# Expert stages of a transformer kernel: tokens sorted by expert through DRAM, 46 tiles of 256 places instead of eight dense experts

## The reference

```python
logits = x @ router_w.T                               # 8 experts
routing_weights, selected = sparsemixer_eval(logits)  # two experts a token
dense_w.at[tok, selected[:, k]].add(routing_weights[:, k])
for e in range(E):
    h = silu(x @ w_gate[e].T) * (x @ w_up[e].T)       # 128 -> 256
    out = out + dense_w[:, e:e + 1] * (h @ w_down[e].T)
```

## Time and profile before

| | us |
|---|---|
| median of 3 runs | 1792.99 (1792.24 to 1793.76) |
| span of the profiled execution | 1790.5 |
| PE busy | 1635.4 |
| DVE busy | 1373.5 |
| ACT busy | 997.7 |
| POOL busy | 342.6 |

### The profile page before, as it was taken

How to read it: one execution, slowest core, us unless ns; L and a number is a source line. 1 busy time by engine, 2 the same in 40 slices (tenths; PEclk the granted TensorE clock), 3 DMA queues, 4 the chain that set the end, 5 groups by cost and what they waited for, 6 DMA issues and landing times.

```text
span 1790.5 us, 30396 instructions
## 1 busy us (share of the span) xinstructions
PE 1635.4 (91%) x10929; PEld 954.7 (53%) x10929; DVE 1373.5 (77%) x2257; ACT 997.7 (56%) x1974; POOL 342.6 (19%) x742
## 2 busy tenths in 40 slices
PE   5899999978999999999999889999999687999687
PEld 5788888721111111111111237788888566666476
DVE  5755555689999999999999447655577796788895
ACT  3223323437888888888888863333322564655463
POOL 5311002462000001000000131001000134334221
PEclk9899999978999999999999999999999798999798
DMA  3000000121001010010001001000000000000000
GB/s 131 1 1 0 0 0 19 53 71 55 23 28 30 29 38 22 23 37 23 23 29 38 8 4 57 1 0 0 0 0 1 1 1 1 2 2 2 1 20 28
DMA packets 25302, 35.93 MB, mean 20 GB/s; under 512 B 5808, under 2 KB 19696, under 8 KB 24672
## 3 DMA queue, kind: packets, MB, share of 16 engines
q1 hardware_dynamic: 25184, 34.38, 6.4%
HBM read 22.57 MB, written 8.78 MB: 18 GB/s over the span
## 4 chain that ended last, share of the span: by engine, by line
PE 76%; DVE 11%; ACT 5%; issue 4%; POOL 2%; DMA 0%; SPq 0%; POOLq 0%; ACTq 0%; DVEq 0%
PE PS L971 14%; PE PS L440 12%; PE PS L959 10%; PE PS L429 7%; PE PS L430 6%; PE PS L431 6%; PE PS L948 5%; ACT probs L1043 3%; DVE neg_half L1106 3%; PE PS L1557 3%; PE PS L1645 2%; PE PS L1655 1%; PE PS L1588 1%; PE PS L1566 1%; PE PS L329 1%
## 5 line engine op out<-in xcount | busy, mean ns | idle before, releaser
L1106 DVE TENSOR_REDUCE neg_half<-PS 128x2 f32<-128x1024 f32 x512 | 601.5, 1219 | 39.5 <-PE PS L948 24.4
L1043 ACT ACTIVATE probs<-PS 128x512 f32<-128x512 f32 x1024 | 528.9, 603 | 112.3 <-PE PS L959 112.2
L523 ACT ACTIVATE shared<-PS 128x512 f32<-128x512 f32 x256 | 152.6, 597 | 374.1 <-PE PS L431 361.2
L959 PE MATMUL PS<-qk_all 51*128 51x512 bf16 x1024 | 279.7, 387 | 17.6 <-ACT probs L1043 12.4
L617 DVE TENSOR_TENSOR shared<-shared,PS 128x512 f32<-128x512 f32 x256 | 174.0, 686 | 156.2 <-ACT shared L523 154.5
L971 PE MATMUL PS<-probs,Vg 128*32 128x512 f32 x2048 | 274.5, 608 | 0.1
L440 PEld LDWEIGHTS PS<-wd,shared 128*128 128x128 f32 x2048 | 249.3, 193 | 11.2 <-issue 0.5
L959 PEld LDWEIGHTS PS<-qk_all 51*128 51x128 bf16 x1024 | 71.6, 93 | 338.3 <-ACT probs L1043 319.3
L440 PE MATMUL PS<-wd,shared 128*128 128x128 f32 x2048 | 250.7, 276 | 0.0
L948 PE MATMUL PS<-qk_all 48*128 48x512 bf16 x1024 | 193.8, 390 | 17.4 <-DVE neg_half L1106 15.3
L625 DVE SCALAR_TENSOR_TENSOR x<-PS,gates,x 128x128 f32 (+1 forms) x512 | 144.0, 343 | 71.6 <-PE PS L440 71.6
(11 more groups left out here) (213 smaller groups left out, 2061.2 us busy)
## 6 DMA issues: line engine op xcount, KB each, us to landing
split<-qk_all SPq DMA_DIRECT2D x16, 384.0 KB, 3.3
qk_all<-split SPq DMA_DIRECT2D x64, 96.0 KB
qk_all<-split SPq DMA_DIRECT2D x64, 64.0 KB
qk_all<-split SPq DMA_DIRECT2D x64, 32.0 KB
shared<-OTs SPq DMA_DIRECT2D x60, 32.0 KB
probs<-in_ret_const SPq DMA_DIRECT2D x1, 1538.5 KB, 6.8
qk_all<-negT SPq DMA_DIRECT2D x96, 4.0 KB, 1.7
SC<-inverse SPq DMA_DIRECT2D x3, 512.0 KB, 4.9
```

The lines of the kernel that those rows point to most:

```text
L523: act.activation(sg[:, f, :], bank(f), ACT.Silu).then_inc(s["silu"], 1)
L959: pe.matmul(bank(RING_AT + use % RING), qs[rows, slot, 1, pair, kt * P:(kt + 1) * P], qs[rows, slot, 0, pair, half * GW:(half + 1) * GW], ...
L1043: act.activation(probs[:, n % 2, STRIPS * strip + pair, :], bank(RING_AT + use % RING), ACT.Exp, scale=ATT_SCALE).then_inc(s["exped"], 1)
L1106: dve.tensor_reduce(neg_half[m % 2][:, i % 2, :, at], bank(use_bank(i, m), 2).rearrange("p (s w) -> p s w", s=STRIPS), AX.X, ALU.max, nega ...
```

## The change

Each expert stage is cut into two parts of 2048 tokens. For each part DVE routes, PE counts the members of each expert with two matmuls, and DVE turns the counts into a place for each token and choice: each expert gets whole tiles of 256 places, 23 tiles a part in every case, 46 a stage. POOL scatters the normalised tokens (`tokens_all`) by indirect DMAs into rows of a DRAM array `slots_x`, one DMA for each token tile and choice, 32 a part. Then each tile runs through one expert: SP reads the expert's number into a register, fetches that expert's weights (384 KB) into a ring of three, and loads the tile's rows (128 KB); PE turns them, runs gate and up as 4 plain fp32 matmuls of 256 columns and down as 4 of 128 columns; ACT copies the result out, and SP stores it to `slots_y`. POOL gathers the two results of each token by indirect DMAs (8 a group, 64 a stage), and DVE adds them to `x` with their weights (`moe_add`). The dense weights in SBUF, their high and low parts and the loops over groups and experts are gone; the tiles are written out.

The second part's gathers and adds are moved: those of stage 0 into turn 0 of the attention, those of stage 2 into the feed-forward stage. Groups 4 to 7 are normalised for the attention by DVE (`LATE_TOKENS`) in place of POOL.

```diff
+SLOTS_TILE = 256
+PARTS_MOE = 2
+PART_TILES = (2 * PART_TOKENS + EXPERTS * (SLOTS_TILE - 1)) // SLOTS_TILE
+STAGE_TILES = PARTS_MOE * PART_TILES
+RING_TILES = 3
...
+        def moe_scatter(pool, n, part, lo=0, hi=PART_TOKEN_TILES):
+            pool.wait_ge(moe["place"], parts_before(n) + part + 1)
+            for t in range(part * PART_TOKEN_TILES + lo, part * PART_TOKEN_TILES + hi):
+                for k in range(2):
+                    pool.indirect_dma_start(slots_x[part][:, :], bass.IndirectOffsetOnAxis(place[:, k, t:t + 1], 0),
+                                            tokens_all[:, t, :], None).then_inc(moe[f"scattered{part}"], 16)
...
+        def moe_load_weights(sp, n, i):
...
+            e = sp.value_load(expert_of[0:1, part, i % PART_TILES:i % PART_TILES + 1], min_val=0, max_val=EXPERTS - 1)
+            wait(sp, moe["y_ps"], k - RING_TILES + 1)
+            sp.dma_start(w_ring[:, r, :], a["w_experts"][bass.ds(e, 1), :, :].rearrange("o p w -> (o p) w")).then_inc(moe[f"w{r}"], 16)
...
+        def moe_store_slots(sp, n, i):
...
+            sp.wait_ge(moe["y"], k + 1)
...
+        def moe_sp(sp, n, at_tile=None, between=None):
+            AHEAD = RING_TILES - 1
...
+            for i in range(STAGE_TILES):
+                if i + AHEAD < STAGE_TILES:
+                    moe_load_weights(sp, n, i + AHEAD)
+                    moe_load_slots(sp, n, i + AHEAD)
+                moe_store_slots(sp, n, i)
...
         def moe_pe(pe, n):
...
+            for i in range(STAGE_TILES):
+                if i + 2 < STAGE_TILES:
+                    turned(i + 2)
+                if i + 1 < STAGE_TILES:
+                    gate_up(i + 1)
+                down(i)
...
+        LATE_ADDS, LATE_TOKENS = {5: 4, 10: 5, 14: 6}, {7: 4, 12: 5, 15: 6}
...
+                if n == 3 and g < PART_GROUPS:
+                    moe_add(dve, 2, PART_GROUPS + g, "late")
```

More of the change, by code:

```diff
@@ L208, in macaron @@
         gn = sb("gn", [P, 2])
[L211 to L215, removed]
+        ld = stage_sems(ctx, nc, "ld", "fp4 ret wret x_first x_second x_rest small ident half att ones ident_b filled stored")
+        ln = stage_sems(ctx, nc, "ln", "stats link rstd late")
+        moe = stage_sems(ctx, nc, "moe", "xn xT_ps xT logit_ps logits shifted exped weighed members counts experts place scattered0 scattered1 "
+                         "w0 w1 w2 in0 in1 in2 out0 out1 out2 in_ps inT gu silu0 silu h y_ps y came0 came1 half_added x_acc")
+        att = stage_sems(ctx, nc, "att", "xn xT_ps xTf q_ps k_ps qkf_half v_ps v_raw qkf rest1 part2 parts V to_dram0 to_dram1 strips filled read neg_step "
                     "neg_p neg_rows scoredT exped pad Vg pv evac moved sums inverse spread moved_last rec on proj biased added neg")
@@ L361, in b @@
             def b(v):
                 return v.unsqueeze(2).to_broadcast([P, N, EXPERTS])
-            S, G, A, F, D, O1, O2, M = (v[:, t, :] for v in (scores, gates, size, factor, below, first, second, masked))
+            S, A, F, D, O1, O2, M = (v[:, t, :] for v in (scores, size, factor, below, first, second, masked))
             K, X = ([v[:, k, t, :] for k in range(2)] for v in (kept, shifted))
-            m, mu = ([v[:, k, t] for k in range(2)] for v in (largest, mult))
+            m = [largest[:, k, t] for k in range(2)]
@@ L403, in route @@
[L403 to L413, removed]
@@ L552, in moe_act, with result @@
+            def result(i):
+                k = tile_of(n, i)
+                act.wait_ge(s["y_ps"], k + 1)
+                wait(act, s[f"out{k % RING_TILES}"], 16 * (k // RING_TILES))
+                act.activation(slots_out[:, k % RING_TILES, :], bank(1)[:, 0:SLOTS_TILE], ACT.Copy
+                               ).then_inc(s["y"], 1)
+            if n == 0:
+                for g in range(HEAD_GROUPS):
+                    moe_copy(act, n, g)
             moe_exp(act, n, 0)
+            for g in range(HEAD_GROUPS, GROUPS):
+                moe_copy(act, n, g)
@@ L554, in moe_act @@
+            moe_exp(act, n, 1)
             act.activation(sg[:, 0, 0:1], ident[:, 0:1], ACT.Silu).then_inc(s["silu0"], 1)
-            act.wait_ge(s["silu0"], 1)
-            group(0, False)
-            with act.Fori(1, GROUPS - 2 if n == 0 else GROUPS - 1) as g:
-                group(g, False)
+            act.wait_ge(s["silu0"], n // 2 + 1)
+            turned(0)
+            turned(1)
+            silu(0)
+            for i in range(STAGE_TILES):
+                if i + 2 < STAGE_TILES:
+                    turned(i + 2)
+                if i + 1 < STAGE_TILES:
+                    silu(i + 1)
+                result(i)
+                if n == 0:
+                    prep_act_at(act, i - PART_TILES)
```

813 lines of the change are left out of this document (419 added, 394 removed).

## The result

The change makes the kernel slower: 2264.8 us (median of 4 runs, 2260.8 to 2269.4) against 1793.4 us, a ratio of 1.263 (95% interval 1.260 to 1.265). The forecast was 2334 us in a range of 2080 to 2530. The profiled execution has a span of 2259.0 us against 1790.5, so 468.5 us have to be found.

What follows compares the result with a forecast made beforehand. PE was taken as the bound. Tiles 984 less dense steps 648, plus heads 68 and 68, turn 0 49 and feed-forward 20, gave +541 us on a 1790.5 us span, about 2334 us; range 2080 to 2530.

Steps and rivals of the forecast that it cites:

- The ring: Expert tiles: next rows' load waits on the result three tiles back; period 10.7 us, 984 us for 92 tiles; low-clock case 0.70.
- The stall: PE idle after every down, through copy, store, register read, weights' issue and rows' landing: 5.0 us a tile.
- The register read: SP reading a tile's expert number, inside the stall: 0.8 us, plus 0.1 us for three register instructions.
- The clock: PE's granted clock falls to its lower level in each stall, making a tile's work 5.7 us instead of 2.85.
- the sign that the prediction had named: A stretch of some 20 us inside an expert stage should show PE busy about half, at a clock near 0.5.
- The heads: Starts of stages 0 and 2, where tiles wait for places and 32 scatters of 1.29 us: +68 us each.
- Turn 0: Attention's turn 0, lengthened by POOL's gathers, preparation and layer norms: 105 against 55.5 us, +49 us; strips shorter than these.
- Feed-forward stage: Four DVE adds with their waits lengthen this stage by 20 us; POOL's gathers fit beside it.
- The full clock: Rival in the expert tiles: clock holds through the stall, period 7.9 us, time 2076 us; chance 0.13.
- Loads ahead of PE: Rival in the expert tiles: rows land as asked for, PE sets a 2.95 us period, time 1621 us; chance 0.03.
- The longer stall: Rival in the expert tiles: register read 1.7 and rows 4.1 us, stall 7.4, period 13.1, time 2555 us; chance 0.13.
- Cheap or dear scatters: Rival on POOL's scatter issue: at 0.45 us each any case is 81 us less, at 2.14 us as much more.

Runs made afterwards that it cites:

- e3: Changed kernel with gate and up of the next tile ahead of the following tile's transposes on PE, silu ahead of the copy on ACT: 1982.0 us.
- e4: Changed kernel with four buffers instead of three for weights, rows and results: 1805.9 us, ratio 1.003 to the kernel before.
- e11: Changed kernel with four buffers, rows ahead of weights, both ahead of the store, register read ahead of the waits, first prepared group's store one tile later: 1675.2 us.
- e9: Changed kernel with unused filler matmuls ahead of stage 2's transposes and a constant expert number instead of the register read: 2160.0 us.
- e1: Changed kernel with each tile's expert a program constant instead of a number read into an SP register: 2262.8 us.
- e7: Changed kernel with six matmuls of unused result ahead of each tile's transposes, in stage 2 only: 2187.9 us.
- e10: Changed kernel with only each token's first choice scattered, 16 indirect DMAs a part instead of 32: 2232.5 us.
- e12: e11 with turn 0 reordered: adds of groups 4 and 5 earlier on DVE, last gathers ahead of splitting the maxima on POOL: 1670.7 us.
- e8: Changed kernel with the second prepared group's store and turn 0's strip load issued behind tile 43's store instead of the last: 2264.9 us.
- e5: Changed kernel with SP issuing a later tile's loads ahead of the store, register read still behind the wait for down: 2239.1 us.
- e6: e5 with the register read made ahead of the wait for down: 2138.4 us.

## Why the prediction was right, and where it wasn't

**The ring: right, and shown.** The stall was forecast at 5.0 us and is 4.9 in the tile shown, 5.05 in the median: copy 0.38 (forecast 0.39), store 0.36 and 0.05 between two issues (0.45), read and registers 0.7 to 0.76 (0.9), weights 0.35 and 0.05 (0.45), next transposes 2.9 behind the start of the rows' issue (2.7 for the landing and 0.1 for waking PE, which no run shows apart). That the order makes it, not the transfers, is shown by e3 (same loads, 283 us less), e4 and e11.

**The register read: right in size.** The Trainium skill, "DMA: Bandwidth & Descriptors", section "Latency and other measured facts", gives a floor of about 600 ns for `tensor_load`. By the gap of 0.76 us, less 0.05 for a plain gap between issues, the trace lies a little above it, with three register instructions in the 0.71 us; 0.54 us of it reach the period in e9. By the floor the forecast would have been 18 us nearer, but e1 shows that in this kernel the price of the read alone changes nothing.

**The clock: right that it falls, wrong in how much of a tile it takes.** The term that was mis-sized is "I take each tile as run at the low level", 5.7 us of PE work. It measured 5.06 us in the tile shown and about 5.1 in the median: gate and up and the transposes at the lower level, `down` mostly at the upper. So the clock of the stages is 0.67 to 0.70, not near 0.5, the sign that the prediction had named. e7 shows the price, 2.02 us a tile against the forecast's 2.85. The period in the middle of a stage is 10.2 us, not 10.7, 46 us over 92 tiles. The other 30 us of the miss are the ends of each stage, where the transposes of the first tiles find their loads landed and nothing behind the last transposes waits for a load: 92 x 10.2 = 938, against 907.6 measured. I had counted every tile as one in the middle. The errors partly cancel: 76 us too much for the tiles, 5 for the heads and 4 for the feed-forward stage, 11 too little for turn 0; the sum is 72 us off.

**The heads: right.** 64.5 and 66.2 us, forecast 68 each. The first scatter starts at 38.42 (forecast 40), 32 take 40.6 us (41); in stage 2 the first starts 15.5 us behind the old start (16):

```profile
38.42 1.21 POOL L472 DMA_INDIRECT slots_x<-tokens_all,place  x1 [10.60 <-DVE place L465]
39.94 0.97 POOL L472 DMA_INDIRECT slots_x<-tokens_all,place  x1 [0.30 <-issue]
```

Taking POOL's price for a tile of 512 columns, 1.29 us, was a guess that met the 0.96 + 0.30 us. The Trainium skill, same page and section, puts the first byte of a GpSimd DMA at about 1 us; by it the forecast of the heads would have been 19 us shorter, and too short, since the trace shows 0.96 us of issue, but also the 0.30 us between two. e10 shows that the scatters hold the head, down to some 16 of them.

**Turn 0: about the right number by a partly wrong chain.** +60.2 against +49. The forecast called the strips hidden beneath POOL's gathers. The chain of turn 0:

```profile
538.54 3.30 DMA split<-qk_all
...
549.12 8.39 DMA qk_all<-split
557.64 0.62 PE PS L1007 x2
558.29 23.45 DVE neg_half L1165 x21
...
583.27 1.06 DVE x L501 x4
...
615.02 1.02 POOL came L487
```

The strips come first (22 us from the last `down` to the first maximum), then 25 us of maxima that stand ahead of the first late add on DVE, and only the last eight gathers are in the chain. e12 bears out that the order on DVE and POOL holds part of it, 6 us; how short turn 0 can get stays open, and what earlier strips would give was not tried far enough by e8.

**Feed-forward stage:** +16.4 against +20 (12.5 to 17.2 over all traces); how it splits into adds and waits, no run here shows.

**The rivals.** The full clock did not hold; e7 shows that with it the period in stage 2 is 8.16 us (forecast 7.9). Loads ahead of PE, the rival on the other side, is what e11 builds: period 2.84 us (forecast 2.95) and 1675 us (forecast 1621; the last twelve tiles of stage 0, among which the attention's preparation and its waits for POOL stand, take 41 us more than that period, most of the rest). The longer stall did not come: the rows land 3.0 us behind their issue, not 4.1, and the read takes 0.7, not 1.7. Cheap or dear scatters did not come either, at 1.26 us apiece.

## What to carry to other kernels

A ring of buffers is as long as the chain that fills a slot, not as its count: write down what each load waits for, and behind what it stands in its queue, and compare with the work between. Here three buffers cost 10.2 us a tile and four, with loads ahead of stores, 2.84. Price short stalls of PE with their clock: a microsecond saved from a stall can be lost to a longer stay at the lower clock, so a null result of one small edit doesn't show that its cost was absent. And look at which ready work stands behind the wait: swapping two calls, on PE and on ACT, was worth 283 us.

## What the runs showed that was not expected

The stall and the clock are coupled. With PE's median wait for the rows at 5.05, 4.64 and 4.42 us a tile (the change, e1 and e5) the period stays between 10.06 and 10.19 us; at 3.84 us (e6) some tiles run at the full clock and the period drops to 6.8 us in those.

The clock also moves the profiled spans: the attention's last 41 us ran at 1.00 in the trace of the change and at 0.78 in e8's, where the other turns are 8 us longer, all of it in the last turn, which takes 58.6 us there against 50.4 (from the first of its 128 matmuls of 128x512 to the last). The trace of e1 has the change's last turn, the other ten have e8's (58.3 to 59.2 us). Spans of single executions should not be compared below that; the +1.7 us of the other turns above hold such a difference too, since in the trace of the kernel before the last turn takes 53.1 us at 0.94.

```profile
1273.03:1314.43 41.40, 33.89 (x231) 1.00 0.02 4
```

```profile
1274.80:1316.60 41.80, 36.53 (x199) 0.78 0.02 4
```
